# Tiles of every fourth row, and neighbour words by accumulating matmuls

## The chip, the core and the metric

The kernel runs on one core of one Trainium2 chip. A core has a matrix engine (TensorE, "PE" in the profile), a vector engine (DVE), a scalar engine (ACT), a general engine (GpSimd, "POOL"), a queue engine (SyncE, "SP") and 16 DMA engines that they share. The metric is the time of one launch on the device in microseconds; lower is better.

## The reference

Two graph layers run over 8 graphs of 2048 nodes with 256 channels. `adj` is a symmetric 0/1 matrix for each graph, with the diagonal set.

```python
h = relu(layernorm(x))
# layer 0: the first S = 25 neighbours of every node, by index
scores = where(adj != 0, -arange(N), -inf)
vals, idx = top_k(scores, S)
agg = h[idx].max(over the 25)           # rows with 25 or fewer neighbours: also max with 0
x = x + relu(concat(h, agg) @ W + b)
# layer 1: attention over all neighbours
h = relu(layernorm(x)); hidden = h @ W1.T
s = leaky_relu(a1.hidden_n + a2.hidden_m, 0.2)
out = softmax(where(adj > 0, s, s - 1e12)) @ hidden + bias
x = x + out
```

## The kernel before, in words

The 16384 rows are cut into 32 quads of 512 rows (`QUADS`, `QR`); a quad is T = 4 tiles of P = 128 rows, and a graph is QB = 4 quads. In the kernel before, row `t * 128 + p` of a quad lies in partition p of tile t. The access patterns `quad` and `tile` (lines 140 and 141) say so for every array: `x`, `out`, and the DRAM scratch arrays `table` (normalised rows for the gathers), `xmid` (x between the layers) and `nmask` (the mask in bf16). A partition moves runs of one row, 1 KB for 256 float32 channels.

One step s of the loop (`step`, one copy for every engine) works on several quads at once, in stages: the index stage for quad s+1, the gathers of quad s, the projection of quad s-1, and the attention of quad a = s-4 (`LAG`). `STEPS` gives the range of s for each stage. Attention runs in steps 4 to 30, the index stage in steps -1 to 30; the last quads are written out by hand in `last_quad`. The order of work on each engine is the order of the code, and the engines meet only through semaphores.

*Index stage.* ACT makes the mask of non-edges from `adj` (`index_masks`, line 507): nm_t is 0 for an edge and 2^40 for none, bf16, two tiles (a "pair", u = 0 and 1) at a time, and sends it to `nmask`. The neighbours must then be found by index, lowest first. Eight columns of a row make one word: PE transposes nm_t in eight blocks of 128 x 128 (`index_transpose`, line 1213), ACT copies the bank to nm_x (`index_half`, line 520), and PE multiplies each block by pack_w, whose 16 columns hold the powers of two (`index_pack`, line 1226). That is done in four halves for a pair, each with the hops PE, ACT, PE; bank1 holds the transposes and bank2 the words. `index_prep` runs the four halves of pair 0 at the start of a step. Those of pair 1 are interleaved with attention chunks 0 to 3. DVE turns the words into keys (`index_words`, line 785), and finds the first 32 words with neighbours and then the first 32 neighbours by rounds of max8 and match_replace8 (`index_rest`, `top_rounds`, lines 769 and 775), and writes `idx`.

*Gather stage.* For each tile, POOL issues 25 indirect DMAs of 128 rows into near[t % 2] (line 464). Before tile n it waits until `agg` of tile n-2 is made, since near has two halves. DVE reduces the 25 rows to a maximum (`maximum`, lines 831 and 834), PE multiplies (`layer0`, lines 1248 to 1258), ACT copies in between (`cat_copy`, line 625), and DVE adds the residual (`residual0`, line 844).

*Attention stage.* For quad a, eight chunks c, of two blocks of 128 columns each. PE adds the mask and the row maxima in PSUM (`penalty`, lines 1301 and 1304), ACT forms the linear part (`leaky`, line 550), DVE adds them (`exponents`, line 918), ACT takes exp (`weights`, line 555), and PE multiplies with the hidden rows (`products`, line 1315). `penalty` of chunk c+1 stands ahead of `products` of chunk c.

On DVE a step is in this order: index_words of pair 0, maximum of tile 0, attend_setup, maximum of tile 1, chunk 0, index_rest of pair 0 with chunk 1 in its middle, chunks 2 and 3, maximum of tile 2, index_words of pair 1, chunk 4, residual of tile 2, chunks 5 to 7, maximum of tile 3, attend_end, statistics, index_rest of pair 1. On PE it is:

```python
if "index" in stages:
    index_prep(s + 1, 0)
if "project" in stages:
    project(s - 1)
gathered(0)
if "attend" in stages:
    attend_setup(a)
gathered(1)
if "index" in stages:
    index_transpose(s + 1, 1, 0)
for c in range(4):
    if "attend" in stages:
        chunk(a, c)
    if "index" in stages:
        if c < 3:
            index_transpose(s + 1, 1, c + 1)
        index_pack(s + 1, 1, c)
gathered(2)
```

## Time and profile before

| | |
|---|---|
| time, median of 3 runs | 6122.58 us (6121.67 to 6129.22) |
| the profiled execution: its own time, its span | 6100.12 us, 6098.2 us |
| PE busy, matmuls | 2809.4 us (46%), 13660 |
| DVE busy | 2965.5 us (49%) |
| ACT busy | 1482.1 us (24%) |
| POOL busy | 3220.2 us (53%), 3200 of them gathers |
| mean granted TensorE clock | 0.667 of full speed |

Busy time leaves out what an engine spends on waits, registers and on issuing DMAs. The idle time before an instruction is put down to what released it; "issue" means that the profile shows nothing that the engine waited for, and "remote" or "another core or an unknown queue" that it does not know the releaser. The granted clock is 1.0 at 2.4 GHz and 0.5 at 1.2 GHz. A row of the table of windows gives a stretch of the span in us, its length, and for each engine the busy us with the number of instructions in brackets.

### The profile page before, as it was taken

Reading aid. Unit: us, or ns where it says so; the run is one execution under the profiler, and the core shown is the slowest. Engines: PE = TensorE matmul, PEld = TensorE weight load, DVE = VectorE, ACT = ScalarE, POOL = GpSimd, SP = SyncE. Lnnn points to the kernel's source line nnn. Section 1 sums busy time; section 2 is a strip of 40 time slices with the busy share of each in tenths; the row PEclk is TensorE's granted clock in tenths of the full one; section 3 lists DMA queues with packets and bytes.
Section 4 is the critical chain, followed back from the end, with each engine's and each line's share of the span. In section 5 each row is a group of like instructions: output and inputs, shape, how many; then the busy total and the mean of one; then the engine's idle time right before and its main releaser. Section 6 shows DMA issues by size and latency. Waiting matters only on the chain.

```text
span 6098.2 us, 48051 instructions
## 1 busy us (share of the span) xinstructions
PE 2809.4 (46%) x13660; PEld 1905.1 (31%) x13660; DVE 2965.5 (49%) x6428; ACT 1482.1 (24%) x1739; POOL 3220.2 (53%) x3204
## 2 busy tenths in 40 slices
PE   2222254444444444543445445454444445454569
PEld 1111132323333233332323323332233333233346
DVE  4333444554445543555534555444554445554555
ACT  2111122222222221222222222222222222222224
POOL 4666655454555545455455554455554555654640
PEclk9555566666666666666666666666666666666679
DMA  6444443443434444344433444343443434443330
GB/s 234 142 131 131 140 140 115 144 152 126 138 102 144 154 140 129 106 137 154 141 123 113 133 154 140 120 131 123 147 148 122 137 110 142 154 138 119 128 105 25
DMA packets 326675, 809.37 MB, mean 133 GB/s; under 512 B 59445, under 2 KB 175034, under 8 KB 310202
## 3 DMA queue, kind: packets, MB, share of 16 engines
q0 software_dynamic: 153600, 419.64, 23.0%
q1 hardware_dynamic: 154586, 321.93, 14.9%
q10 hardware_dynamic: 18432, 67.12, 2.9%
q8 instruction: 28, 0.46, 0.0%
q14 instruction: 29, 0.24, 0.0%
HBM read 691.00 MB, written 119.54 MB: 133 GB/s over the span
## 4 chain that ended last, share of the span: by engine, by line
PE 29%; issue 25%; another core or an unknown queue 23%; DVE 12%; ACT 7%; POOL 4%; ACTq 1%; DMA 0%; DVEq 0%; SPq 0%; POOLq 0%; PEldq 0%
PE acc L1315 14%; DVE near L831 4%; POOL near L464 4%; DVE lin L852 3%; PE bank L1256 3%; PE pen L1304 2%; PE bank L1213 2%; PE acc L1278 2%; PE bank L1272 2%; PE pen L1301 2%; ACT nm_x L520 1%; ACT nm_t L507 1%; PE acc L1265 1%; ACT acc L653 1%
## 5 line engine op out<-in xcount | busy, mean ns | idle before, releaser
L464 POOL DMA_INDIRECT near<-table_dram,idx x3200 | 3220.0, 1006 | 2661.7 <-DVE agg L834 1627.0
L1315 PE MATMUL acc<-hid,wgt 128*128 (+1 forms) x4096 | 1192.1, 437 | 537.7 <-issue 507.6
L918 DVE SCALAR_TENSOR_TENSOR wgt<-pen,a_slope,lin 128x512 f32<-128x512 f32 x512 | 368.3, 747 | 1875.5 <-remote 1681.2
L1315 PEld LDWEIGHTS acc<-hid,wgt 128*128 128x128 f32 x4096 | 877.1, 219 | 791.7 <-issue 658.1
L831 DVE TENSOR_TENSOR near<-near 128x3072 f32<-128x3072 f32 (+3 forms) x512 | 865.3, 1690 | 119.2 <-DMA near<-table_dram,idx 100.4
L520 ACT ACTIVATE nm_x<-bank 128x1024 bf16<-128x1024 bf16 x256 | 261.8, 1023 | 2175.9 <-remote 1705.6
L1213 PE MATMUL bank<-ident_b,nm_t 128*128 128x128 bf16 x2048 | 207.2, 262 | 1108.1 <-ACTq L522 674.2
L550 ACT ACTIVATE lin<-a_b,a_rise 128x512 f32<-128x512 f32 x468 | 322.4, 719 | 1018.0 <-DVE wgt L918 888.6
L769 DVE MAX8 top<-key 128x8 f32<-128x256 f32 x1024 | 390.9, 416 | 361.0 <-remote 228.3
L1213 PEld LDWEIGHTS bank<-ident_b,nm_t 128*128 128x128 bf16 x2048 | 161.6, 118 | 1164.1 <-ACTq L522 624.3
L1256 PE MATMUL bank<-w_sb,h_t 128*128 128x256 f32 x1024 | 379.5, 535 | 182.5 <-ACT h_t L625 148.1
L1301 PE MATMUL pen<-m_r,ones_b 3*128 3x512 bf16 x468 | 214.0, 457 | 463.4 <-DVE wgt L918 391.0
L1304 PE MATMUL pen<-neg_ident,nm_q 128*128 128x128 bf16 x1856 | 243.5, 250 | 333.9 <-issue 333.6
L1256 PEld LDWEIGHTS bank<-w_sb,h_t 128*128 128x128 f32 x1024 | 260.4, 267 | 266.3 <-issue 173.8
L775 DVE MATCH_REPLACE8 key<-top,key 128x256 f32<-128x256 f32 x768 | 309.5, 409 | 0.0
L852 DVE CUSTOM_DVE_ANT_0 lin<-acc,nm_q 128x2048 bf16<-128x2048 f32 x108 | 247.4, 2291 | 68.0 <-ACT acc L653 65.2
L1304 PEld LDWEIGHTS pen<-neg_ident,nm_q 128*128 128x128 bf16 x1856 | 129.0, 107 | 476.6 <-issue 476.5
L555 ACT ACTIVATE wgt<-wgt 128x1024 f32<-128x1024 f32 x256 | 266.8, 1042 | 29.9 <-DVE wgt L918 29.9
L625 ACT ACTIVATE h_t<-bank 128x512 f32<-128x512 f32 x128 | 75.7, 592 | 724.3 <-PE bank L1250 716.9
L507 ACT ACTIVATE nm_t<-adj_i,big_c 128x2048 bf16<-128x2048 int32 x128 | 248.9, 1992 | 7.9 <-DMA adj_i<-in_adj_dram 7.6
L1301 PEld LDWEIGHTS pen<-m_r,ones_b 3*128 3x128 bf16 x468 | 43.8, 94 | 557.4 <-DVE wgt L918 437.0
L1248 PE MATMUL bank<-cst,h_q 128*128 128x128 f32 x256 | 64.1, 339 | 305.3 <-DVE agg L834 292.1
(146 smaller groups left out, 2420.7 us busy)
## 6 DMA issues: line engine op xcount, KB each, us to landing
adj_i<-in_adj_dram SPq DMA_DIRECT2D x128, 1024.0 KB
nmask_dram<-nm_t ACTq DMA_DIRECT2D x128, 512.0 KB
nm_q<-nmask_dram SPq DMA_DIRECT2D x29, 2048.0 KB
near<-table_dram,idx POOLq DMA_INDIRECT x3200
h_q<-table_dram SPq DMA_DIRECT2D x32, 512.0 KB
x_q<-in_x_dram SPq DMA_DIRECT2D x32, 512.0 KB
xmid_dram<-x_q SPq DMA_DIRECT2D x32, 512.0 KB
o_q<-xmid_dram SPq DMA_DIRECT2D x32, 512.0 KB
```

Of the source, the lines that this page charges most:

```text
L464: pool.indirect_dma_start(out=near[:, t % 2, k, :], out_offset=None, in_=table, in_offset=bass.IndirectOffsetOnAxis(ap=idx[:, t, k:k + 1], ...
L520: nc.scalar.activation(nm_x[:, half % 2, :], bank1_b[:, :], ACT.Copy).then_inc(nmx_made, 1)
L550: nc.scalar.activation(lin[:, i, :], row, ACT.Relu, bias=a2_rise[:, j:j + 1], scale=RISE).then_inc(lin_made, 1)
L769: nc.vector.max(top[:, u, 8 * r:8 * r + 8], src[:, u, :]).then_inc(ix_step, 1)
L831: nc.vector.tensor_tensor(rows[:, lo:count, :], rows[:, lo:count, :], rows[:, other:other + count, :], ALU.max).then_inc(mx_step, 1)
L852: nc.vector.tensor_tensor_reduce(out=scratch, in0=scores, in1=non_edges[:, t, :], scale=1.0, scalar=-3.0e38, op0=ALU.subtract, op1=ALU.max ...
L918: nc.vector.scalar_tensor_tensor(wgt[:, c % 2, i * QR:(i + 1) * QR], pen[:, i, :], a2_slope[:, j:j + 1], lin[:, i, :], ALU.add, ALU.add).t ...
L1213: mm = nc.tensor.transpose(bank1_b[:, i * P:(i + 1) * P], nm_t[:, u, j * P:(j + 1) * P], ident_b[:, :])
L1256: nc.tensor.matmul(bank2[:, 0:C], cat_t[:, k * P:(k + 1) * P], w0_sb[:, k, :], start=(k == 0), stop=False)
L1301: nc.tensor.matmul(pen[:, i, :], ones_b[:, :], maxima, start=True, stop=False, skip_group_check=True)
L1304: mm = nc.tensor.matmul(pen[:, i, t * P:(t + 1) * P], non_edges[:, t, j * P:(j + 1) * P], neg_ident[:, :], start=False, stop=(t == T - 1), ...
L1315: mm = nc.tensor.matmul(acc[:, t, 0:C + 1], wgt[:, c % 2, i * QR + t * P:i * QR + (t + 1) * P], hid[:, bass.ds(batch * NJ + j, 1), 0:C + 1 ...
```

## The change

Tiles take every fourth row: row `4 * p + t` of a quad lies in partition p of tile t. A partition then holds four rows that are neighbours in DRAM, and a quad moves in runs of 4 KB (16 KB for the mask). So that the mask's columns stand in the order in which the hidden rows lie, ACT writes nm_t regrouped: within each quad of columns, by t and then r, reading every fourth element of `adj_i`.

The words are no longer made by transposes. bit_w[:, k, :] is the identity times -(2^k)/2^40, and eight matmuls, one for each bit k, accumulate in bank2 the words of a pair: 512 columns each, 2 tiles x 256 words, whose moving operand takes the members k of all words from the regrouped mask, every second bf16 element. nm_x, pack_w, index_transpose, index_pack and index_half go. For pair 1 the eight matmuls stand behind chunk 3 and ahead of layer0 of tile 2. `packed` counts pairs now; ACT waits for it before it overwrites nm_t. DVE's index_words waits for it too, in place of b2_full.

```diff
-    quad = lambda ap, q: ap[bass.ds(q * QR, QR), :].rearrange("(t p) c -> p t c", p=P)
-    tile = lambda ap, q, t: ap[bass.ds(q * QR + t * P, P), :]
+    quad = lambda ap, q: ap[bass.ds(q * QR, QR), :].rearrange("(p t) c -> p t c", t=T)
+    tile = lambda ap, q, t: quad(ap, q)[:, t, :]
...
-        pack_w = sb("pack_w", [P, P // GB], BF16)
+        bit_w = sb("bit_w", [P, GB, P], BF16)
...
-            nc.scalar.activation(pack_w[:, :], cst[:, C_PK:C_PK + P // GB], ACT.Copy).then_inc(set_act, 1)
+            for k in range(GB):
+                ins = nc.scalar.activation(bit_w[:, k, :], ident, ACT.Copy, scale=-(2.0 ** k) / BIG)
+            ins.then_inc(set_act, 1)
...
                     if not (first and pair == 0):
                         act.wait_ge(nm_out[u], 16 * (2 * q + pair))
-                    nc.scalar.activation(nm_t[:, u, :], adj_i[:, u, :], ACT.Relu, bias=BIG_B, scale=-BIG
-                                         ).then_inc(nm_made, 1)
+                        act.wait_ge(packed, 2 * q + pair)
+                    by_tile = adj_i[:, u, :].rearrange("p (q r t) -> p q t r", q=QB, t=T)
+                    nc.scalar.activation(nm_t[:, u, :].rearrange("p (q t r) -> p q t r", q=QB, t=T), by_tile,
+                                         ACT.Relu, bias=BIG_B, scale=-BIG).then_inc(nm_made, 1)
...
-            def index_words(q):
+            def index_words(q, pair):
 
                 words = bank2[:, :].rearrange("p (u g) -> p u g", u=2)
-                dve.wait_ge(b2_full, b2.next())
+                b2.next()
+                dve.wait_ge(packed, 2 * q + pair + 1)
...
+            def index_prep(q, pair):
+
+                pe.wait_ge(nm_made, T * q + 2 * pair + 2)
+                pe.wait_ge(b2_free, b2.next())
+                members = nm_t[:, :, :].rearrange("p u (q t g h) -> p (u q) t g h", q=QB, t=T, h=GB // T)
+                words = bank2[:, :].rearrange("p (b g) -> p b g", b=2 * QB)
+                for k in range(GB):
+                    mm = nc.tensor.matmul(words, bit_w[:, k, :], members[:, :, k % T, :, k // T],
+                                          start=(k == 0), stop=(k == GB - 1))
                 mm.then_inc(packed, 1)
...
                 gathered(1)
-                if "index" in stages:
-                    index_transpose(s + 1, 1, 0)
                 for c in range(4):
                     if "attend" in stages:
                         chunk(a, c)
-                    if "index" in stages:
-                        if c < 3:
-                            index_transpose(s + 1, 1, c + 1)
-                        index_pack(s + 1, 1, c)
+                if "index" in stages:
+                    index_prep(s + 1, 1)
                 gathered(2)
```

The last quads load `nmask` in two DMAs in place of one, and where scratch lay in nm_x it now lies in bits and nm_t.

## Rows read from the trace of the kernel before

**Rows 1.** The page's chain that ended last, share of the span by engine.

```profile
PE 29%; issue 25%; another core or an unknown queue 23%; DVE 12%; ACT 7%; POOL 4%; ACTq 1%; DMA 0%; DVEq 0%; SPq 0%; POOLq 0%; PEldq 0%
```

**Rows 2.** Windows of one quad: PE, PEld, DVE, ACT, POOL, granted clock, DMA share, GB/s.

```profile
2968.40:2999.80 31.40, 6.46 (x58) 4.92 (x56) 13.11 (x49) 6.47 (x5) 23.74 (x25) 0.65 0.75 249
2999.80:3022.70 22.90, 11.10 (x56) 7.81 (x56) 18.69 (x42) 8.41 (x10) 0.00 (x0) 0.65 0.15 53
3022.70:3056.00 33.30, 20.97 (x89) 12.82 (x87) 28.74 (x58) 12.81 (x17) 26.57 (x23) 0.65 0.64 212
3056.00:3089.80 33.80, 5.92 (x23) 2.48 (x20) 7.04 (x24) 2.39 (x3) 25.52 (x27) 0.56 0.36 105
3089.80:3110.80 21.00, 17.29 (x96) 12.89 (x97) 9.92 (x9) 7.67 (x9) 0.00 (x0) 0.74 0.02 6
3110.80:3141.80 31.00, 15.46 (x75) 9.74 (x73) 4.69 (x8) 5.31 (x7) 23.64 (x25) 0.78 0.34 102
3141.80:3158.10 16.30, 10.82 (x45) 8.25 (x46) 10.13 (x10) 3.38 (x4) 0.03 (x1) 0.69 0.39 137
```

**Rows 3.** Timeline of POOL: start, duration, instruction [idle before <- releaser].

```profile
3022.72 0.94 POOL L464 DMA_INDIRECT near<-table_dram,idx  x1 [23.27 <-DVE agg L834]
...
3110.83 0.94 POOL L464 DMA_INDIRECT near<-table_dram,idx  x1 [21.09 <-DVE agg L834]
...
3158.07 0.94 POOL L464 DMA_INDIRECT near<-table_dram,idx  x1 [16.30 <-DVE agg L834]
```

**Rows 4.** Timeline of DVE in the same period, same columns.

```profile
3095.50 1.41 DVE L918 SCALAR_TENSOR_TENSOR wgt<-pen,a_slope,lin 128x512 f32<-128x512 f32 x2 [31.67 <-remote]
3101.40 1.41 DVE L918 SCALAR_TENSOR_TENSOR wgt<-pen,a_slope,lin 128x512 f32<-128x512 f32 x2 [4.49 <-PE pen L1304]
3102.72 6.86 DVE L831 TENSOR_TENSOR near<-near 128x3072 f32<-128x3072 f32 x4
...
3111.29 0.69 DVE L785 SCALAR_TENSOR_TENSOR key<-bank,cst 128x512 f32<-128x512 f32 x1 [1.25 <-PEq L1232]
...
3119.40 0.75 DVE L918 SCALAR_TENSOR_TENSOR wgt<-pen,a_slope,lin 128x512 f32<-128x512 f32 x1 [2.23 <-remote]
3146.24 1.41 DVE L918 SCALAR_TENSOR_TENSOR wgt<-pen,a_slope,lin 128x512 f32<-128x512 f32 x2 [26.09 <-remote]
```

**Rows 5.** Timeline of PE in the same period, same columns.

```profile
3055.40 0.61 PE L1213 MATMUL bank<-ident_b,nm_t 128*128 128x128 bf16 x8
3055.85 0.27 PE L1226 MATMUL bank<-pack_w,nm_x 128*128 128x16 bf16 x5
...
3058.70 0.37 PE L1301 MATMUL pen<-m_r,ones_b 3*128 3x512 bf16 x1 [0.56 <-issue]
...
3094.57 4.92 PE L1315 MATMUL acc<-hid,wgt 128*128 x10 [0.81 <-issue]
3099.29 1.06 PE L1213 MATMUL bank<-ident_b,nm_t 128*128 128x128 bf16 x8
3100.14 0.40 PE L1226 MATMUL bank<-pack_w,nm_x 128*128 128x16 bf16 x8
...
3105.36 0.61 PE L1213 MATMUL bank<-ident_b,nm_t 128*128 128x128 bf16 x8
3105.81 0.35 PE L1226 MATMUL bank<-pack_w,nm_x 128*128 128x16 bf16 x8
```

**Rows 6.** Timeline of ACT in the same period, same columns.

```profile
3036.27 0.60 ACT L564 ACTIVATE a_b<-bank 128x512 f32<-128x512 f32 x1 [7.07 <-PE bank L1286]
```

**Rows 7.** The page's costliest groups: busy, mean ns, idle before them.

```profile
L1301 PE MATMUL pen<-m_r,ones_b 3*128 3x512 bf16 x468 | 214.0, 457 | 463.4 <-DVE wgt L918 391.0
...
L507 ACT ACTIVATE nm_t<-adj_i,big_c 128x2048 bf16<-128x2048 int32 x128 | 248.9, 1992 | 7.9 <-DMA adj_i<-in_adj_dram 7.6
```

**Rows 8.** The page's DMA queues: packets, MB, share of 16 engines.

```profile
q1 hardware_dynamic: 154586, 321.93, 14.9%
q10 hardware_dynamic: 18432, 67.12, 2.9%
```

More of the change, by code:

```diff
@@ L87, in shape_constants @@
     c[:, C_POW:C_POW + GB] = 2.0 ** np.arange(GB)
-    for m in range(P):
-        c[m, C_PK + m // GB] = -(2.0 ** (m % GB)) / BIG
     for q in range(QUADS):
@@ L129, in bank1_uses @@
 def bank1_uses():
-    return Uses(attend=2, gather=T, index=4 * T // 2, project=1)
+    return Uses(attend=2, gather=T, project=1)
 def bank2_uses():
@@ L512, in index_masks @@
                     act.dma_start(tile(nmask, q, t), nm_t[:, u, :]).then_inc(nm_out[u], 16)
-            def index_half(q, pair, half, first):
-                h = 4 * pair + half
-                act.wait_ge(b1_full, b1.next())
-                if not (first and h < 2):
-                    act.wait_ge(packed, 2 * T * q + h - 1)
-                nc.scalar.activation(nm_x[:, half % 2, :], bank1_b[:, :], ACT.Copy).then_inc(nmx_made, 1)
-                act.wait_ge(nmx_made, 2 * T * q + h + 1)
-                act.sem_inc(b1_free, 1)
             def normalise(q, first_col, src, dst, ready, made):
@@ L677, in _ @@
             index_masks(0, 0, True)
-            for half in range(4):
-                index_half(0, 0, half, True)
             act.wait_ge(first_ready, 1)
@@ L684, in _ @@
             index_masks(0, 1, True)
-            for half in range(4):
-                index_half(0, 1, half, True)
             normalise(0, 0, x_ln, h_ln, ln1_ready, h_made)
```

68 lines of the change are left out of this document (16 added, 52 removed).

## The prediction

> **What bounds the kernel now.** I read the page first, then the table of windows over one period of the steady loop, then the timelines of POOL, DVE, PE and ACT in that period, and last the costliest groups. The page's chain gives no engine more than 29%; half of it is "issue" and an unknown releaser [rows 1]. So the period has to be read. One quad takes 189.7 us, and the seven windows of [rows 2] cut it where POOL's gathers start and stop. POOL issues 25 gathers in a burst of about 31 us, four bursts a quad, two of them back to back (3022.7 to 3089.8). Three gaps lie between the bursts, and each ends with the DVE maximum that frees half of near: 23.3, 21.1 and 16.3 us [rows 3], together 60.7 us. The quad's time is the bursts, 129 us, plus these gaps. A change moves the time only if it moves a burst or a gap.
>
> What fills the gaps is the second thing to see. During a burst the other engines crawl: from 3056.0 to 3089.8 PE issues 23 matmuls, 1.47 us each, and in the next 21.0 us, with POOL silent, 96 [rows 2]. DVE waits 31.7 us before its chunk 2 (the first L918 of [rows 4]), until PE runs freely again at 3094.57 [rows 5]. DMA is only 0.36 busy meanwhile [rows 2], so the data path is not what is full. The work left over from a burst is done in the gap behind it. Gap 2 (3089.8 to 3110.8) is: rest of products(1), transposes and packs, penalty(3), DVE chunk 3, then the maximum of tile 2.
>
> **The change, part by part.** The four transposing groups, the four ACT copies and the four packing groups of each pair go. Per quad that is 64 transposes, 64 packs, 8 ACT copies, and every semaphore hop between them. In come 2 x 8 accumulating matmuls with 512 columns.
>
> PE's own time hardly changes. A pair of tiles costs four times 0.45 us (transposes, 3105.36 to the packs at 3105.81) and 0.2 us of packs at the high clock, four times 0.85 us (3099.29 to 3100.14) and up to 0.35 us at the low one [rows 5]: 2.6 to 4.8 us. Eight 512-column bf16 matmuls cost at most 8 x 0.457 = 3.7 us by L1301, which has the same 512 columns and type but 3 rows [rows 7], and at least what the transposes need per column: 1024 columns in 0.45 us [rows 5], so 4096 in 1.8 us. Near enough equal; but 128 matmuls with their weight loads become 16.
>
> Gap 2, direct part: the eight transposes at 3099.29 and the packs at 3100.14 stand ahead of penalty(3), for which DVE waits 4.49 us (L918 at 3101.40, rows 4). The two groups hold PE for 0.85 + 0.40 = 1.25 us. In the crawl, the transposes at 3055.40 and the packs hold PE for 3.3 us, up to penalty(2) at 3058.70 [rows 5]; freed, that is two matmuls more of products(1) at 1.47 us each, which otherwise take 0.3 to 0.5 us each in the gap: 0.6 us. Sure part: 1.9 us.
>
> Gap 2, second part: PE enters the crawl at about 3056 and has to issue, from the first index group of chunk 0 to the end of penalty(3), 102 matmuls: 24 transposes, 16 packs, three penalties of 10 and two products of 16. 47 are out by then (8 transposes, a penalty, products, 8 transposes and the 5 packs at 3055.85 in [rows 5]). Without the index work the stretch holds 62; if those 47 still get out, 15 are left, 22 us at 1.47 us each, and penalty(3) is done before PE is freed. DVE then no longer waits for it: chunk 2 at 3095.50 to 3096.9, ACT's linear part of chunk 3 to 3098.0, DVE chunk 3 to 3098.6, the maximum at 3098.6 in place of 3102.7 [rows 4]. That is 4.1 us. I take this over the 1.9 us, since the matmuls that crawl are counted, and their number falls by 40%.
>
> Gap 1 (2999.8 to 3022.7): DVE is the engine that works in it, 18.7 of 22.9 us [rows 2], at index_rest and the maximum, none of which changes. ACT loses four copies and hops in front of project, so the projection ends earlier, but DVE comes to its first use of it only behind the maximum that ends this gap, and the maximum of tile 1, next, has the double burst up to 3089.8 as cover. I take 0. Gap 3: chunks 6 and 7 and the maximum, no index work: 0 of itself.
>
> What is moved: the packing of pair 1 now stands as one block behind chunk 3 and ahead of layer0 of tile 2. In the old order DVE's index_words came at 3111.29 after a wait of 1.25 us [rows 4]. Now 1.8 to 3.7 us of matmuls follow products(3), where 0.4 us of packs did, and 1.3 us of transposes and packs between the products before it are gone: index_words, DVE chunk 4, the residual and chunk 5 come up to 2 us later, counted from POOL's restart. POOL's restart itself hangs on the maximum ahead of them, so this costs 0 now; what it may cost later is a rival below. Behind it on PE stand layer0(2) and penalties 5 to 7.
>
> The added waits on packed in index_masks were met long before (pair 0 is packed at the start of a step, the masks of pair 1 are made behind the project stage; pair 1 is packed in mid-step, the next masks are made a step later): 0. The mask ACTIVATE now reads every fourth int32. Its contiguous form takes 1.99 us [rows 7]; no row has a 16-byte step. Lower bound 1.99, upper bound twice that. The pair-1 masks are followed by 7.07 us in which ACT waits for PE [rows 6], so even 4 us more are covered: 0. The Trainium skill (SBUF — State Buffer, Door 1: The DMA port swizzle) says that SBUF reads run at full rate only with two or more hits to a 16-byte line; by that the mask would slow down, to an amount it does not give, and the sum stays as it is while that is under 7 us a pair.
>
> DMA: 224 transfers of 512 KB go from 1 KB runs to 4 KB runs, 114,688 packets to 28,672. By [rows 8] (share x 16 engines x 6098 us, over the bytes) queue 1 spends 46 ns per KB and queue 10, whose data all moves in 4 KB runs, 43 ns; if the whole excess is due to the short runs, 1% of the engines' time is freed, 60 us of each. The gaps end on DVE and not on a transfer [rows 3]: 0, and if the cover were gone at most 60 us.
>
> Sum: 27 quads run with attend and index together, 27 x 4.1 = 111 us off the profiled execution's 6100.1 us: 5989. The median of the runs is 22.5 us above that execution, so 6012 us.
>
> **Rivals.** (a) The crawl does not go by count. If PE's onset keeps its place in the program and not its count of instructions, only the sure part stays: 27 x 1.9 = 51 us, 6071. For it: DVE issues 49, 58, 24 and 8 instructions in the four bursts' windows, so no one count fits it. Against it: PE gets 89 matmuls out in the first half of the double burst and 75 in the single one, and 23 in the half that follows without a gap [rows 2], as if a store of them ran dry. The Trainium skill (Runtime: NRT & Kernel Launch, Instruction fetch mechanics) says fetching is sequential and hidden by the pace of issue except after branches; by that fewer instructions buy nothing but their own time, which is this case. No row here shows fetching itself.
>
> (b) The block behind chunk 3 tips gap 3. DVE's chunk 5 ends at 3120.15 and the next starts only at 3146.24, after 26 us of crawl [rows 4]. Chunk 5 made it by little. If it comes up to 2 us later it may fall into the crawl, and a whole chunk, 5.9 us (from chunk 2 at 3095.50 to chunk 3 at 3101.40), moves into gap 3: 27 x (5.9 - 1.9) = +108, 6231. It decides where the second half of DVE's chunk 5 starts over 8.6 us (3119.40 less 3110.83) after POOL's restart. Against it: PE and ACT have fewer instructions behind them too.
>
> (c) The other way round: ACT and PE get further before the crawl, and chunk 6 or 7 is done ahead of it. Each chunk out of gap 3 gives 5.9 us; both of them beside the 4.1: 27 x 15.9 = 429, 5694. A full closing of gap 2 is worth 21.1 us. For it: ACT loses 8 of its 54 instructions a quad [rows 2] and the waits around them. Against it: DVE, which loses nothing, is stalled at 3120 as well.
>
> (d) No change: the index work was done where PE and ACT stood idle, and gap 2 is then ruled by DVE and ACT alone. Within 12 us of 6123.
>
> **How the numbers follow.** Forecast case (4.1 us a quad, give or take 2): 0.40. (a) 0.20, (c) 0.10, (d) 0.09, (b) 0.21. The time is that of the forecast, 6012 us. The range leaves out (c) at its full size and the upper half of (b), together 2 in 10: 5870 to 6230. Between its ends lie the bounds of the 512-column matmul and the 60 us of DMA. Faster by more than 0.2% (12 us, a bit more than the 7.6 us by which the three runs differ, about what can be told from no change): forecast, (a) and (c), 0.70. Within it 0.09. Slower 0.21.
>
> **What would show it.** In the profile after: the lines of transposes, packs and copies gone, 512 accumulating matmuls of 0.22 to 0.46 us mean in their place. POOL's three idle times per quad: 23 us and 16 us as before, 21 down to 17. DVE's wait for penalty(3) near 0. Wrong would be: gap 3 above 20 us (b), gap 3 near 5 us (c), gap 2 at 19 us (a). A mask ACTIVATE over 5 us or a 512-column matmul over 0.8 us (a strided moving operand, for which no row speaks) would break the step that costs them at nothing.

## The result, and the profile after

| | before | after |
|---|---|---|
| time, median | 6122.12 us (4 runs, 6108.05 to 6129.22) | 5900.40 us (4 runs, 5893.19 to 5906.56) |
| ratio | | 0.964, 95% interval 0.9619 to 0.9662 |
| profiled execution: time, span | 6100.12, 6098.2 us | 5904.69, 5902.8 us |

The forecast was a fall of 111 us to 6012 us, and the fall is 222 us, twice that. 5900 us lies inside the range of 5870 to 6230, and beyond the forecast case's own size.

One quad of the steady loop, cut as in [rows 2] where POOL's gathers start and stop (PE, PEld, DVE, ACT, POOL, clock, DMA share, GB/s):

```profile
2873.10:2905.00 31.90, 15.28 (x46) 8.58 (x46) 15.27 (x57) 12.02 (x9) 24.57 (x25) 0.73 0.80 279
2905.00:2923.70 18.70, 0.60 (x3) 0.60 (x4) 16.29 (x33) 4.91 (x6) 0.00 (x0) 0.53 0.18 63
2923.70:2958.60 34.90, 24.44 (x70) 14.34 (x68) 33.08 (x76) 15.88 (x14) 27.33 (x25) 0.52 0.54 180
2958.60:2989.70 31.10, 5.26 (x26) 3.45 (x25) 1.61 (x7) 0.00 (x0) 23.67 (x25) 0.65 0.36 105
2989.70:3006.00 16.30, 10.43 (x42) 7.06 (x43) 10.01 (x9) 4.56 (x6) 0.00 (x0) 0.63 0.03 8
3006.00:3037.00 31.00, 18.17 (x78) 12.11 (x77) 4.70 (x8) 5.31 (x7) 23.67 (x25) 0.76 0.35 102
3037.00:3054.00 17.00, 14.61 (x48) 10.14 (x48) 10.01 (x9) 3.38 (x4) 0.01 (x1) 0.63 0.36 131
```

The bursts (first, third, fourth, sixth row) take 128.9 us where they took 129.5 [rows 2]. The gaps are 18.7, 16.3 and 17.0 us where they were 23.3, 21.1 and 16.3 [rows 3]. One quad can mislead, so the same was taken as a mean over steps 5 to 26, from the end of a tile's last gather to the start of the next tile's first:

| us | gap 1 | gap 2 | gap 3 | four bursts | period |
|---|---|---|---|---|---|
| before | 22.8 | 20.3 | 16.3 | 128.8 | 188.6 |
| after | 19.3 | 16.2 | 17.2 | 128.5 | 181.5 |
| difference | -3.5 | -4.2 | +0.9 | -0.3 | -7.1 |

22 steps of that are 156 us of the 195.4 us between the two spans. 2.4 us lie before the first gather, 9.7 us in steps 0 to 3 (no attention yet), 9.2 us in step 4, and 18 us in all that follows the start of step 27. The 9.7 us are not spread evenly: step 0 is 17.9 us shorter, since its gap 1 is gone (0.3 us in place of 21.7), and step 1 is 8.1 us longer. Gap 1 also varies from quad to quad after the change: in 18 of the 22 steps it is 16.6 to 19.6 us, in the other four 22.3 to 22.9.

The timeline of DVE through gap 2, after (start, duration, instruction, [idle before <- releaser]):

```profile
2993.10 0.75 DVE L901 SCALAR_TENSOR_TENSOR wgt<-pen,a_slope,lin 128x512 f32<-128x512 f32 x1 [32.81 <-remote]
2995.25 1.41 DVE L901 SCALAR_TENSOR_TENSOR wgt<-pen,a_slope,lin 128x512 f32<-128x512 f32 x2 [1.40 <-PE pen L1263]
2997.24 0.75 DVE L901 SCALAR_TENSOR_TENSOR wgt<-pen,a_slope,lin 128x512 f32<-128x512 f32 x1 [0.58 <-PE pen L1263]
2997.91 6.86 DVE L813 TENSOR_TENSOR near<-near 128x3072 f32<-128x3072 f32 x4
...
3010.20 0.69 DVE L767 SCALAR_TENSOR_TENSOR key<-bank,cst 128x512 f32<-128x512 f32 x1 [4.98 <-PE bank L1196]
...
3020.29 0.75 DVE L901 SCALAR_TENSOR_TENSOR wgt<-pen,a_slope,lin 128x512 f32<-128x512 f32 x1 [3.86 <-remote]
3027.36 0.75 DVE L901 SCALAR_TENSOR_TENSOR wgt<-pen,a_slope,lin 128x512 f32<-128x512 f32 x1 [6.31 <-remote]
3041.73 1.41 DVE L901 SCALAR_TENSOR_TENSOR wgt<-pen,a_slope,lin 128x512 f32<-128x512 f32 x2 [13.62 <-remote]
```

And of PE and ACT in the same quad, from the start of its step on:

```profile
2881.63 3.59 PE L1196 MATMUL bank<-nm_t,bit_w 128*128 128x512 bf16 x8 [5.24 <-ACT nm_t L506]
...
2959.46 0.40 PE L1263 MATMUL pen<-neg_ident,nm_q 128*128 128x128 bf16 x4
...
2967.16 0.38 PE L1274 MATMUL acc<-hid,wgt 128*128 x1 [1.73 <-issue]
2993.91 0.60 PE L1260 MATMUL pen<-m_r,ones_b 3*128 3x512 bf16 x1 [26.37 <-DVE wgt L901]
...
2996.06 0.60 PE L1260 MATMUL pen<-m_r,ones_b 3*128 3x512 bf16 x1 [1.01 <-DVE wgt L901]
...
3008.19 1.98 PE L1196 MATMUL bank<-nm_t,bit_w 128*128 128x512 bf16 x8
```

```profile
2873.62 7.81 ACT L506 ACTIVATE nm_t<-adj_i,big_c 128x2048 bf16<-128x2048 int32 x2
```

Two things are to be seen. DVE's chunk 2 starts at 2993.10, 3.4 us after the burst ended at 2989.7, where it started 5.7 us after it [rows 4: 3095.50 less 3089.8]. And from there to the maximum it is 4.8 us (2997.91) in place of 7.2 us (3102.72). Together 4.7 us, all of the gap's fall in this quad. This split belongs to this quad: over steps 5 to 26 the start of chunk 2 scatters by some 2 us after the change. Measured at chunk 2's second half it holds in the mean. That half starts 5.4 us after the burst in place of 6.3, and from there to the maximum it is 2.7 us in place of 5.9.

The way is shorter because PE has nothing left to do in it. Before, penalty(3) stood behind ten products of chunk 1, eight transposes and eight packs [rows 5: 3094.57 to 3100.54]. After, the last product of chunk 1 is out at 2967.16, 22 us before the burst ends. But penalty(3) is not done early: PE issues its halves at 2993.91 and 2996.06, each behind a half of DVE's chunk 2 (`<-DVE wgt L901`), whose reading frees the buffer, and DVE's rows of 2995.25 and 2997.24 still wait for PE, 1.40 and 0.58 us.

What DVE's chunk 2 needs had long been made: penalty(2) by 2959.9 (the second PE row above), the linear part by 2955.5 and products(0) by 2958.6. Before the change, penalty(2) ended with this row, 17 us before chunk 2 (3095.50):

```profile
3078.44 0.26 PE L1304 MATMUL pen<-neg_ident,nm_q 128*128 128x128 bf16 x1 [3.22 <-issue]
```

In the mean over steps 5 to 26 chunk 2 starts 17.7 us after penalty(2) before the change and 32.3 us after it with the change. So in both kernels DVE itself is held in the crawl there, and it does not wait for PE.

The page's chain by engine, the rows on the new operations, and the queue:

```profile
DVE 38%; another core or an unknown queue 25%; PE 17%; issue 15%; POOL 4%; ACT 1%; DVEq 1%; DMA 1%; POOLq 0%; SPq 0%; ACTq 0%
```

```profile
L506 ACT ACTIVATE nm_t<-adj_i,big_c 128x2048 bf16<-128x2048 int32 x128 | 497.8, 3941 | 5.1 <-DMA adj_i<-in_adj_dram 5.1
...
L1196 PE MATMUL bank<-nm_t,bit_w 128*128 128x512 bf16 x512 | 182.1, 516 | 216.3 <-ACT nm_t L506 117.7
```

```profile
q1 hardware_dynamic: 56298, 321.92, 15.0%
```

DVE has 38% of the chain where it had 12%, and "issue" 15% where it had 25% [rows 1].

### The profile page after: what moved, and what is told of

Read it like the earlier page. It is cut to its first block, busy times and chain, and to the rows that moved or that the text cites. A ratio compares the mean times of both kernels' runs of the same rounds, so it can differ in the third digit from the quotient of the medians.

```text
span 5902.8 us, 39139 instructions
## 1 busy us (share of the span) xinstructions
PE 2747.9 (47%) x10076; PEld 1747.5 (30%) x10076; DVE 2954.6 (50%) x6428; ACT 1472.6 (25%) x1490; POOL 3218.1 (55%) x3204
## 3 DMA queue, kind: packets, MB, share of 16 engines
q1 hardware_dynamic: 56298, 321.92, 15.0%
## 4 chain that ended last, share of the span: by engine, by line
DVE 38%; another core or an unknown queue 25%; PE 17%; issue 15%; POOL 4%; ACT 1%; DVEq 1%; DMA 1%; POOLq 0%; SPq 0%; ACTq 0%
PE acc L1274 11%; DVE near L813 10%; DVE top L750 7%; DVE key L756 6%; POOL near L459 4%; DVE lin L835 3%; DVE wgt L901 2%; PE bank L1215 1%; DVE stat L698 1%; PE pen L1263 1%; PE pen L1260 1%; DVE key L791 1%; PE bank L1196 1%; ACT wgt L544 1%
## 5 line engine op out<-in xcount | busy, mean ns | idle before, releaser
L901 DVE SCALAR_TENSOR_TENSOR wgt<-pen,a_slope,lin 128x512 f32<-128x512 f32 x512 | 366.9, 747 | 1732.4 <-remote 1497.5
L1274 PEld LDWEIGHTS acc<-hid,wgt 128*128 128x128 f32 x4096 | 897.8, 225 | 437.5 <-issue 281.0
L813 DVE TENSOR_TENSOR near<-near 128x3072 f32<-128x3072 f32 (+3 forms) x512 | 865.9, 1691 | 119.4 <-DMA near<-table_dram,idx 101.5
L1260 PE MATMUL pen<-m_r,ones_b 3*128 3x512 bf16 x468 | 227.9, 487 | 1113.6 <-DVE wgt L901 641.1
L506 ACT ACTIVATE nm_t<-adj_i,big_c 128x2048 bf16<-128x2048 int32 x128 | 497.8, 3941 | 5.1 <-DMA adj_i<-in_adj_dram 5.1
L1207 PEld LDWEIGHTS bank<-cst,h_q 128*128 128x128 f32 x256 | 35.1, 176 | 1022.2 <-issue 636.9
L1196 PE MATMUL bank<-nm_t,bit_w 128*128 128x512 bf16 x512 | 182.1, 516 | 216.3 <-ACT nm_t L506 117.7
L1231 PE MATMUL bank<-h_t,wa_b 128*128 128x512 f32 x128 | 118.1, 1077 | 267.8 <-issue 228.3
L1263 PE MATMUL pen<-neg_ident,nm_q 128*128 128x128 bf16 x1856 | 229.8, 262 | 0.0
```

Of the source, the lines that this page charges most:

```text
L506: nc.scalar.activation(nm_t[:, u, :].rearrange("p (q t r) -> p q t r", q=QB, t=T), by_tile, ACT.Relu, bias=BIG_B, scale=-BIG).then_inc(nm_ ...
L813: nc.vector.tensor_tensor(rows[:, lo:count, :], rows[:, lo:count, :], rows[:, other:other + count, :], ALU.max).then_inc(mx_step, 1)
L901: nc.vector.scalar_tensor_tensor(wgt[:, c % 2, i * QR:(i + 1) * QR], pen[:, i, :], a2_slope[:, j:j + 1], lin[:, i, :], ALU.add, ALU.add).t ...
L1260: nc.tensor.matmul(pen[:, i, :], ones_b[:, :], maxima, start=True, stop=False, skip_group_check=True)
L1263: mm = nc.tensor.matmul(pen[:, i, t * P:(t + 1) * P], non_edges[:, t, j * P:(j + 1) * P], neg_ident[:, :], start=False, stop=(t == T - 1), ...
L1274: mm = nc.tensor.matmul(acc[:, t, 0:C + 1], wgt[:, c % 2, i * QR + t * P:i * QR + (t + 1) * P], hid[:, bass.ds(batch * NJ + j, 1), 0:C + 1 ...
```

## The experiments

**A condition of the chip came first.** The experiments ran on six chips. On four of them the kernel before takes 4734 to 4744 us, and not some 6100. None of these six was used a second time, so whether the difference belongs to the chip or to the hour is not shown. Several kernels below put other columns into a word or leave gathers out: they do the same kind of work and do not compute the reference. The first four kernels ran where the kernel before is fast:

- the words alone: the new matmuls, with rows, DMAs and the mask's order as before;

```diff
+    quad = lambda ap, q: ap[bass.ds(q * QR, QR), :].rearrange("(t p) c -> p t c", p=P)
...
+                    nc.scalar.activation(nm_t[:, u, :], adj_i[:, u, :], ACT.Relu, bias=BIG_B, scale=-BIG
+                                         ).then_inc(nm_made, 1)
```

> The accumulating matmuls alone: rows lie in the partitions as before the change (1 KB runs) and the mask is written in plain order, so its ACTIVATE should be back at 1.99 us; the matmuls take the members that the regrouped order would give, so the words hold other columns (the neighbours found are not the reference's) and the work is the same. Theory C (fewer instructions and hops on PE and ACT shift the crawl): both shortened gaps come with it, gap 1 near 19.3 and gap 2 near 16.2 us, time 5895 to 5930. Theory D (the 4 KB runs relieve the stretch in which DVE crawls): only gap 2 is shortened, gap 1 stays at 22.8, time 5990 to 6020.

- the layout alone: rows, DMAs and regrouped mask as after, words by transposes as before;

```diff
+    tile = lambda ap, q, t: quad(ap, q)[:, t, :]
...
+                    nc.scalar.activation(nm_t[:, u, :].rearrange("p (q t r) -> p q t r", q=QB, t=T), by_tile,
```

> The layout alone: 4 KB runs and the regrouped mask with its slower ACTIVATE, but the words by transposes, copies and packs as before (so they hold other columns than the reference's neighbours; the amount of work is the same). Theory C: 6115 to 6150, since nothing of the index work goes and the masks cost ACT 8 us a quad. Theory D: gap 1 falls from 22.8 to about 19.3 us, time 6020 to 6050.

- the changed kernel with the contiguous mask (only the second part of the first diff);

> The changed kernel with the mask written in plain order (the ACTIVATE reads adj contiguously; the attention mask's columns then belong to other rows than the reference's). If the doubled mask (3.94 us) is covered: 5900 within 12 us. If the masks delay the matmuls of pair 0 into DVE's crawl or the row scores behind those of pair 1: 2 us a quad or more, 5840 or less.

- the changed kernel with the removed count of TensorE instructions put back, in `index_prep`.

```diff
+                for k in range(56):
+                    nc.tensor.matmul(bank2[:, 0:16], bit_w[:, k % GB, :], nm_t[:, 0, 0:16], start=True, stop=True)
                 for k in range(GB):
                     mm = nc.tensor.matmul(words, bit_w[:, k, :], members[:, :, k % T, :, k // T],
```

> The changed kernel with 56 matmuls of 16 columns ahead of the eight of each pair, written over by them, so that PE has its 128 index matmuls a quad again without the hops through ACT. If the count of PE's instructions is what matters: most of the gain goes, 6060 to 6150, gap 2 at 19 us or more. If the hops through ACT were what mattered: only the fillers' own time is added, 1.4 to 2.8 us a pair where it lies on the path, 5900 to 5960.

All four: 4736.0, 4735.5, 4730.3 and 4732.1 us against 4734.2 us, ratios 1.0005, 1.0005, 0.9994 and 0.9993, each interval within 0.0011 of its ratio. The cases that the four expectations set apart all suppose the slow issue of engines during gathers (the crawl of the prediction), so these runs decide between none of them. The changed kernel itself was then run alone (4731.0 against 4735.5 us, 0.9993) and with three more on a third chip of that kind: changed 4739.6, filler 4738.3, layout alone 4741.6, and the words with the mask read in its natural order 4739.1, against 4741.1 us.

The natural-order kernel has rows, DMAs and mask as before, and takes the members of a word where they then lie:

```diff
+                members = nm_t[:, :, :].rearrange("p u (g k) -> p (u g) k", k=GB)
+                    mm = nc.tensor.matmul(bank2[:, :], bit_w[:, k, :], members[:, :, k],
```

> The changed kernel itself, unaltered, beside the kernel before on one chip. In the last four runs the kernel before took 4734 us and no engine crawled during POOL's bursts, which run back to back, 140.8 us a quad; the recorded 6122 us had gaps of 60 us a quad. If the crawl is a condition of the chip or of the hour and not of the kernel: either both kernels stand near 4734 us, equal within 0.2%, or both are back near 6122 and 5900. If the change itself matters without the crawl: faster than before by more than 0.2% where before takes 4734 us.

> The changed kernel once more, as the yardstick of the other three on this chip. If the kernel before takes some 6000 us here (engines crawl while POOL gathers): 0.96 to 0.97 of it. If it takes 4734 us: equal to it.

> The matmul words without the layout, computing the reference: rows in the partitions as before the change (1 KB runs), plain mask, and the matmuls read every eighth bf16 (16 bytes apart) in place of every second. With 13 gathers the words alone were worth 151 us and the layout cost 18 us alone and 74 us on top of them. On a crawling chip: 40 to 110 us faster than the changed kernel if the matmul keeps its 0.52 us at that step; slower than it if the 16-byte step doubles the matmul. On a chip that does not crawl: 4734 us.

> The changed kernel with 56 matmuls of 16 columns ahead of the eight of each pair. On a crawling chip, if the count of PE's instructions is what the crawl charges for: most of the gain goes, 60 to 220 us slower than the changed kernel, gap 1 and gap 2 both longer. If the hops through ACT were what was saved: only the fillers' time, up to 40 us. On a chip that does not crawl: 4732 us, as before.

> The layout alone with all 25 gathers (transposes and packs as before, words of other columns). On a crawling chip: 0 to 60 us slower than the kernel before, as with 13 gathers (18 us), if the masks' 3.94 us is all it does; faster than it if the 4 KB runs relieve the stretch in which DVE crawls (gap 1 shorter). On a chip that does not crawl: 4735 us.

Nine runs, none off 1.000 by more than 0.0007. The windows of the changed kernel there say why; the four rows are the four bursts of one quad:

```profile
2146.60:2182.70 36.10, 17.57 (x49) 9.95 (x48) 25.92 (x74) 12.03 (x9) 28.78 (x25) 0.67 0.74 266
2183.00:2217.20 34.20, 13.42 (x42) 7.26 (x40) 24.04 (x45) 15.70 (x13) 26.85 (x25) 0.59 0.69 244
2217.50:2252.40 34.90, 24.72 (x108) 17.22 (x109) 26.06 (x61) 9.59 (x13) 27.54 (x25) 0.72 0.33 94
2252.70:2287.00 34.30, 27.52 (x126) 19.75 (x125) 14.52 (x17) 8.63 (x11) 26.98 (x25) 0.90 0.45 146
```

```profile
POOL near L459 74%; PE acc L1274 2%; PE pen L1263 0%; PE pen L1260 0%; DMA nmask_dram<-nm_t 0%; DMA table_dram<-near 0%; DMA adj_i<-in_adj_dram 0%; DVE near L813 0%; ACT near L665 0%; PE bank L1245 0%; ACT lin L539 0%; ACT nm_t L506 0%; POO
```

The bursts stand 0.3 us apart, and PE issues 325 matmuls in the four with POOL at work all the time, up to 126 in one. On the chip of the result it was 220, up to 78 in one (46, 70, 26 and 78 above), and the rest had to be done in the gaps. So the crawl of the prediction is not what gathers do to a core as such. It was there on some chips and not on others, and where it is missing POOL's issuing is 74% of the chain, the index work is hidden in each of the forms tried, and rival (d) is what happens.

One step that [rows 7] could not price is priced by the natural-order kernel. Its matmuls read their moving operand at a step of 16 bytes, in place of 4:

```profile
L1194 PE MATMUL bank<-nm_t,bit_w 128*128 128x512 bf16 x512 | 471.1, 1076 | 55.8 <-ACT nm_t L505 33.2
```

```profile
L505 ACT ACTIVATE nm_t<-adj_i,big_c 128x2048 bf16<-128x2048 int32 x128 | 249.0, 1992 | 7.8 <-DMA adj_i<-in_adj_dram 7.8
```

1076 ns a matmul where the changed kernel has 516, and the mask back at 1992 ns from 3941. The regrouping buys the one with the other.

**Thirteen gathers a tile.** To see words and layout apart where there are gaps with or without the crawl, kernels with 13 of the 25 gathers were made; their bursts are half as long.

```diff
+SG = 13
...
-                    for k in range(S):
+                    for k in range(SG):
...
+            nc.vector.memset(near[:, :, NJ:S, :], 0.0)
```

> The kernel before with 13 of the 25 gathers of every tile (the maximum still folds 25 rows, of which 12 are stale, so the result differs from the reference): POOL needs half its time, so that where nothing crawls POOL no longer sets the period. Without the crawl: below 4200 us, the period ruled by DVE (91 us busy a quad) and the waits on its path. If the chip crawls: bursts of half the length and crawls of half the length, some 4700 us.

> The changed kernel with the same 13 gathers. Theory C (the hops through ACT and PE's count of instructions lie on the path of the chunks): 3 to 6 us a quad faster than the kernel before with 13 gathers, that is 80 to 160 us. Rival (the index work was done in time that nobody needed, and only the crawl made it cost anything): equal to it within 10 us.

> The matmul words alone (1 KB runs, plain mask, words of other columns) with 13 gathers. Theory C: as the changed kernel with 13 gathers or up to 30 us faster, since the masks cost ACT 2 us less each. Rival: as the kernel before with 13 gathers.

> The layout alone (4 KB runs, regrouped mask, transposes and packs as before, words of other columns) with 13 gathers. Theory C: as the kernel before with 13 gathers, or up to 8 us a quad slower where the masks of 3.94 us stand on ACT's path. Rival (fewer packets free the queues): faster than it.

These four ran on a chip with the crawl (the kernel before, with all 25 gathers: 6010.8 us):

| 13 gathers | time, us | to the first row | gap 1 | gap 2 | gap 3 |
|---|---|---|---|---|---|
| before | 4156.2 | | 22.5 | 18.7 | 14.4 |
| changed | 4078.7 | -77 (0.981) | 21.4 | 13.6 | 20.0 |
| words alone | 4004.7 | -151 (0.964) | 18.5 | 13.6 | 19.7 |
| layout alone | 4173.9 | +18 (1.004) | 21.5 | 18.6 | 14.4 |

The gain is the words', all of it: 151 us. The layout takes 18 us by itself, and 74 us on top of the words. By itself it takes them outside the steady loop: 14 us in steps 0 to 3, while the mean quad of steps 5 to 26 is 0.2 us shorter. On top of the words it takes 3.0 us a quad, 2.9 of them in gap 1. Gap 2 falls by 5.1 us with the words and by 0.1 with the layout. 3.8 of the 5.1 us lie between the second half of chunk 2 and the maximum: 6.6 us before and with the layout alone, 2.7 us with the words and in the changed kernel. Gap 3 grows by 5.3 us with the words, so rival (b) is real where bursts are short. Three of the four expectations missed: the kernel before was put at some 4700 us on such a chip, the changed kernel 80 to 160 us below the kernel before (77 measured), and the words alone at most 30 us below the changed kernel, where they are 74.

Two of the same kind, changed and with the filler, ran without the crawl:

> The changed kernel with 13 of 25 gathers again, as the yardstick of the filler on this chip. On a crawling chip 0.677 of the kernel before, as on the other; on a chip that does not crawl its time shows what DVE and PE need without POOL and without the crawl, some 3300 to 3900 us.

> The changed kernel with 13 of 25 gathers and 56 matmuls of 16 columns more for each pair (stale rows in the maximum). If PE's count of instructions is what the crawl charges for: on a crawling chip 50 to 150 us slower than the changed kernel with 13 gathers. If the hops through ACT were what was saved: within 30 us of it. On a chip that does not crawl: within 30 us of it by either.

3601.5 and 3620.5 us: the 3584 small matmuls cost 19 us there, 0.5%, 5.3 ns each. Without the crawl the count of TensorE's instructions is nearly free.

**The two that settle it, with all 25 gathers and the crawl** (the kernel before: 6110.9 us, 6098.6 to 6115.7).

> The words by matmuls, with the rows, the DMAs and the contiguous mask of the kernel before (the word matmuls read the ungrouped mask at the step of the changed kernel, so that they collect the wrong columns into a word). Same kernel as e1_words_only, drawn for a chip on which the engines crawl during the gathers. There: all of the gain from the words gives at most 0.964 of the kernel before, 0.955 if the slower mask of the changed kernel takes some of it back; gain from the layout: 1.00. Without the crawl: 1.000 as in e1_words_only.

> The changed kernel with its 112 removed TensorE instructions per quad put back as small matmuls without a semaphore, at the places of the old transposes and packs. With the crawl: if PE's place in the crawl goes by the count of its instructions, the gain is lost again (1.00 of the kernel before, or 0.98 for half of it); if it goes by the hops between PE, ACT and DVE, the time stays at 0.964. Without the crawl: 1.000, at most 0.005 slower than the changed kernel.

| | time, us | ratio, 95% interval | gap 1 | gap 2 | gap 3 |
|---|---|---|---|---|---|
| words alone | 5848.7 | 0.9556 (0.9517 to 0.9596) | 17.6 | 16.0 | 17.2 |
| changed + filler | 6255.7 | 1.0256 (1.0227 to 1.0286) | 18.6 | 16.3 | 30.6 |

The words alone do more than the whole change: 0.956 against 0.964. Gap 1 makes the difference, 17.6 against 19.3 us as means. These means hide two values: with the words alone gap 1 is 14.2 to 17.4 us in 16 of the 22 steps and 22.3 to 23.6 in six. The two timelines differ at the start of the step, which is a likely cause. In the changed kernel the masks of pair 0 take 7.81 us on ACT, and the words' matmuls wait 5.24 us for them (the row at 2881.63 above). With the contiguous mask:

```profile
2865.64 3.16 PE L1195 MATMUL bank<-nm_t,bit_w 128*128 128x512 bf16 x8 [1.33 <-ACT nm_t L505]
```

```profile
2861.54 3.90 ACT L505 ACTIVATE nm_t<-adj_i,big_c 128x2048 bf16<-128x2048 int32 x2
```

3.90 us and a wait of 1.33. The kernel that has the contiguous mask as its only difference from the changed one (e3_mask_plain) ran only without the crawl. So it is not shown that the mask, and not the rows and runs of the layout, costs these 1.7 us.

The filler turns 0.964 into 1.026. It has no semaphore, no hop and no ACT copy, only 112 small matmuls a quad, 0.17 us each. Its windows, around the restart behind gap 2:

```profile
3156.20:3172.40 16.20, 9.84 (x38) 6.44 (x39) 10.01 (x9) 4.56 (x6) 0.53 (x1) 0.58 0.05 15
3172.40:3203.40 31.00, 9.78 (x84) 5.84 (x82) 0.00 (x0) 0.00 (x0) 23.08 (x25) 0.68 0.33 97
3203.40:3234.00 30.60, 22.86 (x108) 17.07 (x108) 15.04 (x20) 8.63 (x11) 0.56 (x1) 0.83 0.21 77
```

In the 31.0 us of the burst PE issues 84 matmuls. It was 75 in the kernel before [rows 2] and 78 after. But up to 56 of the 84 are filler: PE is busy for 9.8 us of them and not for 18.2. The timeline of the quad before it shows when the crawl sets in:

```profile
2981.22 1.35 PE L1196 MATMUL bank<-nm_t,bit_w 128*128 128x16 bf16 x48
2982.96 0.27 PE L1196 MATMUL bank<-nm_t,bit_w 128*128 128x16 bf16 x5 [0.39 <-issue]
2983.70 0.17 PE L1196 MATMUL bank<-nm_t,bit_w 128*128 128x16 bf16 x1 [0.47 <-issue]
2984.40 0.21 PE L1196 MATMUL bank<-nm_t,bit_w 128*128 128x16 bf16 x2 [0.54 <-issue]
...
2985.83 2.73 PE L1198 MATMUL bank<-nm_t,bit_w 128*128 128x512 bf16 x6 [0.75 <-issue]
```

POOL restarted at 2978.8. 48 filler matmuls pass at full pace, and at 2982.6, 3.8 us into the burst, the "issue" waits begin. In the kernel before and in the changed one the first such wait on PE is 13 us into it (at 3124.0 and 3019.0, behind restarts at 3110.8 and 3006.0). By then PE has issued 66 and 58 matmuls since the restart, and 59 with the filler. As a mean over steps 6 to 25 the matmuls issued since POOL's restart are:

| us since the restart | 4 | 6 | 14 | 30 |
|---|---|---|---|---|
| before | 19 | 32 | 66 | 73 |
| after | 18 | 24 | 59 | 72 |
| words alone | 18 | 24 | 60 | 74 |
| after + filler | 58 | 67 | 77 | 78 |

The burst's whole yield is 72 to 78 in all four, and some 60 of them pass before the crawl, whether in 4 us or in 13. So what PE gets out at full pace in this burst goes by instructions, and not by time or by hops: a small matmul counts like a large one. The double burst ahead of gap 2 bears it out at another place. There PE's run of "issue" waits begins after 86 to 93 matmuls since the restart in each of steps 6 to 25 of the kernel before, and after 88 to 92 in the changed kernel. But the place in the program moved, from the packs and penalty(2) to the products of chunk 1. The count differs from burst to burst: in the one ahead of gap 1 PE issues 55 matmuls in 30 us before and 44 after. Chunk 4, which the changed kernel had behind it before the crawl, and chunk 5 fall into gap 3 (index_words comes at 3014.19, behind the burst, where it came at 3010.20, 4.2 us into it), and gap 3 grows from 17.2 to 30.6 us. In step 0 the filler gives back the gap 1 that the change took away (21.7 us before, 0.3 after, 21.7 with the filler). In the steady loop it does not (18.6), and neither does it lengthen gap 2 (16.3).

The expectation for a rule by count was 1.00, and 1.026 is beyond it. In the kernel before, the instructions of pair 1 were spread over chunks 0 to 3, ahead of POOL's restart. The filler does not stand where they stood, as its expectation had it: it puts 56 of them in one block at the restart, ahead of chunks 4 and 5. So where an instruction stands counts beside how many there are, and fillers at the old places, which would test gap 2, were not run.

**A version that looks beyond the change.** On the chips without the crawl the bursts are 34 to 36 us long, not 31. The timeline of POOL shows a gather of 3.44 us and one of 1.49 us among gathers of 0.95 us, where DVE's maximum of five two-input steps (L813, from 2152.12 on) runs. These rows are of the changed kernel on such a chip:

```profile
2151.61 0.95 POOL L459 DMA_INDIRECT near<-table_dram,idx  x1 [0.30 <-issue]
2152.86 3.44 POOL L459 DMA_INDIRECT near<-table_dram,idx  x1 [0.30 <-issue]
2156.61 1.49 POOL L459 DMA_INDIRECT near<-table_dram,idx  x1 [0.30 <-issue]
```

```profile
2152.12 6.87 DVE L813 TENSOR_TENSOR near<-near 128x3072 f32<-128x3072 f32 x4 [9.49 <-DMA near<-table_dram,idx]
```

The Trainium skill (SBUF — State Buffer, SBUF: two separate sides) says that a DVE instruction with two SBUF inputs shares a port pair, as a lock, with a GpSimd instruction that reads SBUF. The rows fit: the first of the five steps ends at 2155.5, and the gather that started in it at 2156.3. So the maximum was made with one input, on the words with the mask in natural order (rows and DMAs as before the change):

```diff
-                folds = [(0, 12, 13), (0, 6, 7), (0, 3, 4), (0, 2, 2)]
...
+                nc.vector.tensor_reduce(agg[:, :], rows.rearrange("p k c -> p c k"), axis=AX.X, op=ALU.max
+                                        ).then_inc(agg_made, 1)
```

> h2_natural with the maximum over the 25 rows as one DVE reduction with one input in place of five maxima with two. In all traces a gather of POOL takes 3 to 4 us, and the two behind it 1.4 to 1.5 us, when the first maximum of a tile runs, 4 to 5 us a tile. If two SBUF inputs are what stalls POOL: bursts of 30 to 31 us, on a chip that does not crawl 4 x 4 = 16 us a quad less, 4250 to 4350; on a crawling chip 0 to 5 us a quad less than the changed kernel, since only the second burst holds a maximum. Rival: the reduction reads 1 KB apart and takes twice the 7.3 us of the maxima; without the crawl that is still hidden, with it 15 to 20 us a quad slower than the changed kernel.

4390.8 us against 4744.1, 0.9258 (0.9243 to 0.9273), on a chip without the crawl. The gathers with the reduction, and behind them those of the changed kernel:

```profile
L459 POOL DMA_INDIRECT near<-table_dram,idx x3200 | 3076.4, 961 | 1109.6 <-issue 962.7
L810 DVE TENSOR_REDUCE agg<-near 128x256 f32<-128x6400 f32 x128 | 1405.2, 10978 | 132.1 <-DMA near<-table_dram,idx 128.5
```

```profile
L459 POOL DMA_INDIRECT near<-table_dram,idx x3200 | 3539.5, 1106 | 1012.3 <-issue 975.2
```

The reduction takes 10.98 us where the five steps take 7.3, and yet the kernel gains 353 us, since a gather falls from a mean of 1106 to 961 ns (3200 of them: 463 us). It beats both kernels on such a chip, though it misses the 4250 to 4350 us expected. The bursts are 31 us as expected, but POOL now waits 4.0 us a quad for DVE behind the second burst. With the crawl, where the maximum ends every gap, 3.7 us more in each of three gaps stand against it; that was not run.

## Why the prediction was right or wrong

**Gap 2, direct and second part: the size right, the mechanism half wrong.** 4.1 us were forecast and 4.2 measured, and it is the words that give them (gap 2 is 16.0 us with the words alone; with 13 gathers the layout alone leaves it as it was). The forecast came from 102 matmuls less 40, 47 of which get out. That PE's crawl goes by count is borne out against rival (a): in the double burst it sets in after some 90 matmuls in both kernels, at different places of the program, and in the next burst the filler brings it forward. But the step "penalty(3) is done before PE is freed, DVE then no longer waits for it" failed: penalty(3) cannot run ahead, because its PSUM buffer is freed by DVE's chunk 2. I counted PE's instructions and did not ask what each waits for. What took its place: the way from the second half of chunk 2 to the maximum is shorter by 3.2 us, with the products, transposes and packs ahead of penalty(3) out of it, and that half comes 0.9 us sooner behind the burst. The prediction had also read chunk 2 as waiting until PE runs freely again. Its inputs were ready 17.7 us earlier before the change and 32.3 us after it, so DVE's own crawl sets its start. That the total came out within 0.1 us of the forecast is therefore partly luck.

**Gap 1, "I take 0": the step that failed.** It fell by 3.5 us, 27 x 3.5 = 95 us of the 111 us by which the forecast falls short. The argument was that DVE is the engine at work in this gap and that none of its work changes. That is true of its work and not of its place: the gap holds what DVE has not issued when the burst ends. In [rows 2] DVE issues 49 instructions in the burst ahead of gap 1 and 42 in the gap; after, 57 and 33. As means over steps 6 to 25, DVE issues 50 in the first 30 us of that burst before, 55 after and 63 with the words alone. In that burst DVE crawls from 10.3 us behind POOL's restart on (at 2968.4) before, and from 11.8 us on (restart at 2873.1) after, and the statistics end 15.7 us behind it before and 9.9 us after, as a timeline of each shows:

```profile
2979.11 0.17 DVE L736 SCALAR_TENSOR_TENSOR nwt<-nwt,var 128x8 f32<-128x8 f32 x1 [0.40 <-DVE nwt L734]
2979.82 0.17 DVE L738 SCALAR_TENSOR_TENSOR rstd<-nwt,rstd 128x8 f32<-128x8 f32 x1 [0.55 <-DVE nwt L736]
2980.55 0.17 DVE L734 TENSOR_TENSOR nwt<-rstd 128x8 f32<-128x8 f32 x1 [0.56 <-issue]
2981.97 0.17 DVE L736 SCALAR_TENSOR_TENSOR nwt<-nwt,var 128x8 f32<-128x8 f32 x1 [1.25 <-issue]
...
2984.09 0.17 DVE L740 SCALAR_TENSOR_TENSOR shift<-mv,rstd 128x8 f32<-128x8 f32 x1 [1.25 <-DVE rstd L738]
```

```profile
2883.00 0.17 DVE L721 SCALAR_TENSOR_TENSOR shift<-mv,rstd 128x8 f32<-128x8 f32 x1
...
2885.66 0.43 DVE L750 MAX8 top<-key 128x8 f32<-128x256 f32 x1 [0.81 <-DVE key L756]
```

L740 at 2984.09 and L721 at 2883.00 are the same instruction. The words do this (gap 1: 22.8 before, 17.6 with the words alone). Which of their parts helps DVE, PE's instructions or ACT's four copies with their hops, is open. The filler brings PE's count back and leaves gap 1 at 18.6 us in the steady loop (DVE issues 55 in those 30 us with it), which speaks against PE's count and for the copies and hops; no run has the copies alone.

**Gap 3, 0 of itself, and rival (b).** +0.9 us. The place that the rival named is where it happened: the first half of chunk 5 starts at 3020.29, the second at 3027.36 (14.3 and 21.4 us behind the restart), where both halves were out by 3120.15 [rows 4]. Chunk 5 fell into the crawl but not into the gap, so a fraction of the 5.9 us was paid. With 13 gathers 5.3 us were paid, and with the filler 13.4. The place of this rival was named rightly. Its price was not 5.9 us: by these rows it depends on how long the burst still is. The 8.6 us at which it was to decide was passed without that price.

**The 512-column matmul.** 516 ns against bounds of 0.22 to 0.46 us, out by 13%: the rows of 2881.63 and 3008.19 have 3.59 and 1.98 us for eight, nearly a factor of two, as the transposes had in [rows 5]. The excess over the bound, 0.06 us each and 0.5 us for a block of eight, is small beside the 4.2 us; where the block stands costs more, as said under the added waits.

**The mask's ACTIVATE, 0.** It doubled, to 3941 ns, the upper bound. The reason given for the cover spoke of pair 1, where 7.07 us were free [rows 6]. Pair 0 has none: PE waits for it at the head of the step, and gap 1 is 1.7 us longer than in the kernel with the contiguous mask and the old layout. 27 x 1.7 = 46 us were given back, and the runs agree, though on two chips (0.9556 against 0.964, 0.8%, 51 us). That the mask is the cause is likely and not shown, as said above. This is the step with the Trainium skill's rule (SBUF — State Buffer, Door 1: The DMA port swizzle) of two hits to a 16-byte line; both directions agree with it: ACT reads int32 at 16 bytes 2.0 times as slowly, and TensorE reads bf16 at 16 bytes 2.1 times as slowly as at 4.

**DMA, 0.** Right. Queue 1 went from 154,586 packets to 56,298 and stayed at 15.0% of the engines against 14.9 [rows 8]. By the working of [rows 8] that is 46 ns a KB before and 45 after: a run of 4 KB is hardly cheaper than four of 1 KB, and each engine's time falls from 909 to 885 us, not by the 60 us of the bound. On a chip without the crawl it is 895 us with 1 KB runs (h2_natural) and 853 with 4 KB (h1_after), and the time is the same.

**The added waits, 0.** Nothing in the rows after waits for `packed` on ACT. DVE's index_words waits 4.98 us for L1196 (3010.20) where it waited 1.25: the block of eight stands behind 16 products. Counted from POOL's restart that is 4.2 us and not 0.5 [rows 3, 4], 3.7 us later where up to 2 was forecast. By these rows it is what pushed chunk 5 into the crawl; no run moved the block alone.

**Sum.** Forecast 27 x 4.1 = 111. Measured, by the same 27: gap 2 -113, gap 1 -95, gap 3 +24, bursts -8: -192, against 195 between the spans. The close agreement is in part chance, since steps 5 to 26 give 156 us, the steps with attention outside them and the end 27, and 12 come from before step 4.

## What to carry to other kernels

When engines issue slowly for a stretch, price a removed instruction by what it lets through, for every engine that has work left at the stretch's end, and not only for the one that the instruction ran on. Before a producer is said to run ahead, look for who frees its buffer. An engine whose work does not change can still gain by its place, as DVE did in gap 1. What one quad shows should be checked against the mean of all. A kernel's gain may belong to one chip's condition: here the same change is worth 3.6% on one and nothing on two others, so note the time of an unchanged kernel beside every run.

## What the hardware showed that I had not expected

- The kernel before takes 6122, 6111 and 6011 us on three chips and 4734 to 4744 on four others. The difference is the crawl: on the three, engines issue instructions at steps of about 0.7 us (DVE at 2979.11, 2979.82, 2980.55 and 2981.97 in the rows above), or less often, while POOL issues gathers. What causes it is not shown by any run here. In the trace of the kernel before, the two instruction queues move no packet between 900 and 4900 us, so no loading of code that is recorded there is the cause; whether these queues carry the loading of every engine, the trace does not say.
- For TensorE it begins after a number of instructions and not after a time: in the 20 quads of steps 6 to 25 after 57 to 68 matmuls behind gap 2 in the kernel before, and after 55 to 62 with the fillers, though these are used up in 3 to 6 us in place of 12 to 15. In the double burst it is 86 to 93.
- 128 x 2048 int32 read by ACT at a step of 16 bytes: 3.94 us, contiguous 1.99. 512 columns of bf16 as TensorE's moving operand at a step of 4 bytes 0.52 us, at 16 bytes 1.08.
- Five two-input maxima beside POOL's gathers cost a gather 145 ns on average; beside one tensor_reduce of 10.98 us the mean is 961 ns, with most gathers at 946.
